# Clearing the send buffer of a mixture-of-experts kernel: one fill of the whole buffer, or 128 zero rows behind each expert's last row

## The reference

```python
gate_scores = einsum('bsd,de->bse', x, gate_w) + gate_b          # 24 experts
topk_val, topk_idx = lax.top_k(gate_scores, 2)
sparse_gates = softmax(topk_val)
combine = sum(one_hot(topk_idx, 24) * sparse_gates[..., None], axis=-2)
h = gelu(einsum('bsd,edf->besf', x, w1) + b1)                    # 128 -> 512, each expert
y = einsum('besf,efd->besd', h, w2) + b2                         # 512 -> 128
out = einsum('bse,besd->bsd', combine, y) + x
```

## Time and profile before

| | |
|---|---|
| median of 3 runs | 788.13 us |
| span of the profiled execution (first to last instruction) | 791.8 us |
| PE / DVE / ACT / POOL busy | 81% / 67% / 51% / 52% |
| DMA traffic over the span | 84.4 MB, of it 45.5 MB written to DRAM |
| Mamba stage | scan from 70 us, its last step at 180 us |
| first mixture | first send at 213 us, first slot loaded from 266 us, results read back from 382 us |
| second mixture, behind the attention | first send at 604 us, first slot loaded from 657 us |

### The profile page before, as it was taken

How to read it: one execution, slowest core, us unless ns; L and a number is a source line. 1 busy time by engine, 2 the same in 40 slices (tenths; PEclk the granted TensorE clock), 3 DMA queues, 4 the chain that set the end, 5 groups by cost and what they waited for, 6 DMA issues and landing times.

```text
span 791.8 us, 17837 instructions
## 1 busy us (share of the span) xinstructions
PE 642.2 (81%) x4583; PEld 434.2 (55%) x4583; DVE 529.6 (67%) x1518; ACT 405.3 (51%) x880; POOL 414.8 (52%) x488
## 2 busy tenths in 40 slices
PE   4974888888865599999287799999888648999890
PEld 2311333324653499999143355555456517999890
DVE  6779999996565266555378889899645633665444
ACT  2645777772321165665075567677644303566550
POOL 5203999985667255454277534444444672545450
PEclk9965999999995799999699599999999867999995
DMA  7979999922011122221618311211002112222215
GB/s 205 321 254 256 251 247 249 249 58 80 8 34 47 53 81 70 72 72 41 185 36 287 128 51 49 59 49 35 4 0 98 34 53 58 78 71 67 67 42 166
DMA packets 88312, 84.43 MB, mean 107 GB/s; under 512 B 12897, under 2 KB 77401, under 8 KB 87977
## 3 DMA queue, kind: packets, MB, share of 16 engines
q1 hardware_dynamic: 82600, 71.89, 33.9%
q0 software_dynamic: 5632, 11.58, 4.5%
HBM read 37.98 MB, written 45.46 MB: 105 GB/s over the span
## 4 chain that ended last, share of the span: by engine, by line
PE 33%; DVE 7%; issue 5%; DMA 2%; SPq 2%; ACT 2%; POOL 1%; ACTq 0%; DVEq 0%; POOLq 0%
PE bank L643 7%; PE bank L652 6%; PE bank L2017 5%; PE bank L1948 3%; PE bank L1951 2%; DVE t_peak L1768 2%; PE bank L2127 2%; PE bank L1993 2%; PE bank L2118 1%; DVE X L249 1%; PE bank L636 1%; SPq L1427 1%; DMA work<-results 1%; PE bank L2044 1%; DVE t_tabs L1848 0%
## 5 line engine op out<-in xcount | busy, mean ns | idle before, releaser
L806 POOL TENSOR_TENSOR UN<-work 128x512 f32<-128x512 f32 x64 | 81.7, 1289 | 55.4 <-DVE work L1034 54.7
L1768 DVE TENSOR_REDUCE t_peak<-bank 128x1 f32<-128x512 f32 (+2 forms) x192 | 104.0, 592 | 9.5 <-PE bank L1951 7.4
L445 ACT ACTIVATE t_v_tiles<-bank,t_e_b1all 128x128 f32<-128x128 f32 x224 | 64.0, 368 | 63.5 <-PE bank L643 58.8
L445 ACT ACTIVATE m_dx_tiles<-bank,m_e_b1all 128x128 f32<-128x128 f32 x224 | 64.0, 369 | 60.0 <-PE bank L643 57.8
L410 POOL DMA_INDIRECT results<-t_A,t_e_to_row x56 | 53.8, 961 | 67.1 <-DVE t_A L559 33.0
L410 POOL DMA_INDIRECT results<-m_XC,m_e_to_row x56 | 53.8, 961 | 63.7 <-issue 33.9
L1181 PE MATMUL bank<-UN,ident 128*128 128x512 f32 x128 | 71.0, 637 | 14.2 <-POOL UN L806 13.6
L1034 DVE TENSOR_TENSOR_SCAN work<-bank,work 128x512 f32<-128x512 f32 x64 | 76.6, 1216 | 8.3 <-POOL UN L806 7.0
L549 DVE COPY UN<-w1all 128x512 f32 x112 | 48.2, 430 | 40.5 <-PE bank L643 28.4
L652 PE MATMUL bank<-w2all,t_v_tiles 128*128 x448 | 60.6, 279 | 2.7 <-ACT t_v_tiles L445 2.0
L643 PE MATMUL bank<-t_A,UN 128*128 128x128 f32 x448 | 61.0, 280 | 0.0
(11 more groups left out here) (323 smaller groups left out, 1441.8 us busy)
## 6 DMA issues: line engine op xcount, KB each, us to landing
xrows<-m_nothing SPq DMA_DIRECT2D x25, 1032.0 KB, 17.9
w1all<-in_e_w SPq DMA_DIRECT2D x6, 1024.0 KB, 12.2
work<-results SPq DMA_DIRECT2D x16, 256.0 KB, 4.5
m_dx_tiles<-xrows SPq DMA_DIRECT2D x56, 64.5 KB
t_v_tiles<-xrows SPq DMA_DIRECT2D x56, 64.5 KB
t_tabs<-stacks SPq DMA_DIRECT2D x32, 96.0 KB, 2.2
work<-stacks SPq DMA_DIRECT2D x32, 96.0 KB, 2.1
m_tabs<-in_e_b SPq DMA_DIRECT2D x1, 1536.0 KB
```

The costliest lines, as they stand in the source:

```text
L445: ins = act.activation(e.hid[:, mp, f * P:f * P + P], core.tiles(2 + mp)[:, f, :], ACT.Gelu, bias=row(e.b1all, x)[:, f:f + 1])
L806: g.tensor_tensor(hc[:, k % 4, :], h[:, k % 2, :], c_sb[:, k % 2, :], ALU.mult).then_inc(hc_ready, 1)
L1768: v.tensor_reduce(peak[p][:, a, ss[0]:ss[-1] + 1, qt], bank[:, f, 0:len(ss) * w].rearrange("p (j n) -> p j n", n=w), AX_X, ALU.max).then_i ...
```

## The change

SP's 25 fills of 1 MB are gone. Each layer now clears only the 128 rows behind each expert's last row, 24 transfers of 66 KB, once the counts are known.

- DVE gets one more instruction in each layer: `end_row` = count + region base, 24 numbers, in front of the chain that works out the slots. It signals `end_row_ready`.
- SP clears for the experts with even numbers and ACT for those with odd numbers (`clear_ends`): wait for `end_row_ready`, then twelve times a `value_load` of the row number and a DMA from `nothing` to `xrows`. On SP this stands in front of the wait for `sent`; on ACT it stands in front of the exponential of the gates (`gexp`).
- SP then waits for `zeroed` to reach the count of all transfers of this layer, before it loads the first slot. POOL's wait for `zeroed` is gone.
- One more static transfer clears the 128 rows that all unused slots now read: `first_row` is capped at that row (DVE, same place, another operation).
- A region is 2176 rows instead of 2048, the buffer 52,352 rows instead of 56,320, and `nothing` is one row of 129 floats per partition, kept over both stages.

The diff, without the declarations of new tiles and semaphores:

```diff
-REGION = NB * T
-XROWS = NE * REGION + SLOT_TILES * P
-ZERO_ROWS = 2
-ZERO_LOADS = NE + 1
+REGION = NB * T + P
+XROWS = NE * REGION + P
...
+    def clear_ends(self, eng, experts):
+        e, core = self, self.core
+        eng.wait_ge(e.end_row_ready, 1)
+        for x in experts:
+            r = eng.value_load(e.end_row[0:1, x:x + 1], min_val=0, max_val=XROWS - P)
+            eng.dma_start(core.xrows[bass.ds(r, P), :], core.nothing[:]).then_inc(core.zeroed, 16)
+
     def sync(self, sp):
         e, core = self, self.core
+        e.clear_ends(sp, range(0, NE, 2))
+        sp.wait_ge(core.zeroed, 16 + 16 * NE * e.layer)
         sp.wait_ge(core.sent, 16 * TOPK * NT * e.layer)
         sp.wait_ge(e.first_row_ready, 1)
...
         if b == 0 and k == 0 and 0 in tiles:
-            g.wait_ge(e.core.zeroed, 16 * ZERO_LOADS)
             g.wait_ge(e.numbered, TOPK)
...
     def scalar(self, act):
         e, core = self, self.core
+        e.clear_ends(act, range(1, NE, 2))
         act.wait_ge(e.gdiff_ready, 1)
...
         count = bank[0:SLOT_TILES, 6, 0:NE]
+        v.tensor_tensor(e.end_row[:], count[0:1, :], e.base_e[0:1, :], ALU.add).then_inc(e.end_row_ready, 1)
...
-        v.tensor_copy(e.first_row[:], begins[0:1, :]).then_inc(e.first_row_ready, 1)
+        v.tensor_scalar(e.first_row[:], begins[0:1, :], float(NE * REGION), None, ALU.min).then_inc(e.first_row_ready, 1)
...
-            for x in range(ZERO_LOADS):
-                rows = core.xrows[x * REGION:min(x * REGION + REGION, XROWS), :]
-                n = rows.shape[0] // P // ZERO_ROWS
-                sp.dma_start(rows.rearrange("(p a r) d -> p a (r d)", p=P, r=ZERO_ROWS),
-                             nothing[:].unsqueeze(1).to_broadcast([P, n, ZERO_ROWS * ROW])).then_inc(core.zeroed, 16)
+            sp.dma_start(core.xrows[NE * REGION:, :], core.nothing[:]).then_inc(core.zeroed, 16)
```

More of the change, by code:

```diff
@@ L71, in __init__ @@
         self.zeroed, self.sent = self.sem("zeroed"), self.sem("sent")
+        self.nothing = self.sb("nothing", [P, ROW])
         self.results = nc.dram_tensor("results", ((TOPK * NT + SLOT_TILES) * P, D), F32).ap()
@@ L280, in __init__ @@
         self.owner, self.first_row = sb("owner", [1, SLOT_TILES], I32), sb("first_row", [1, SLOT_TILES], I32)
+        self.end_row = sb("end_row", [1, NE], I32)
         self.filled, self.emptied = sb("filled", [P, SLOT_TILES]), sb("emptied", [P, SLOT_TILES])
@@ L322, in __init__ @@
         self.gdiff_ready, self.gexp_ready, self.gate_step = map(sem, ("gdiff_ready", "gexp_ready", "gate_step"))
-        self.stored = sem("stored")
+        self.stored, self.end_row_ready = sem("stored"), sem("end_row_ready")
         self.slot_turned, self.xsT_ready, self.w1_ready, self.mm1_done, self.gelu_done = \
@@ L680, in mamba @@
     X1 = core.XN
-    nothing = st.sb("nothing", [P, ZERO_ROWS * ROW])
     spare = core.UN[:].rearrange("p t d -> p (t d)")
@@ L790, in _ @@
                 g.memset(x[:, 0:NCONV - 1], 0.0).then_inc(edge_set, 1)
-            g.memset(nothing[:], 0.0).then_inc(nothing_set, 1)
+            g.memset(core.nothing[:], 0.0).then_inc(nothing_set, 1)
             g.wait_ge(core.consts_set, 1)
```

## The result

The changed kernel takes 790.43 us (median of 20 runs, 787.79 to 793.8), the kernel before 786.29 us beside it (783.64 to 789.38). The ratio is 1.0051 (95% interval 1.0038 to 1.0065): about 4.0 us slower, where no change was forecast.

A forecast was written before the change was run, and what follows sets the result against it. POOL's sends were taken to bound both mixtures' beginnings. Fills 0 (−0.3 at best), DVE 0 and hidden transfers 0 summed to 0 us against the profiled 791.8 us, 788.1 us for the runs' median; range 786.0 to 792.5 us.

The forecast's parts named there:

- What bounds the kernel: Beginning of both mixtures: POOL's sends end last, not the row numbers; SP and PE go on together after the last lands.
- The fills cost nothing: Scan: nobody waits for a fill, so removing them gives 0, at best −0.3 us.
- The sign that I had set against this term: Scan on POOL: rounds shorter than 6.9 us without the fills would mean the fills' term failed.
- DVE: Slots' chain: `end_row` adds 0.20 us a layer, covered by sends that end 13 us later; sum 0.
- The issuing: SP and ACT queues: first clear after 1.75 us, then 1.10 us each, hidden with 1.5 us to spare; cost 0.
- Do the DMA engines carry it?: Clears beside sends: a clear takes 0.27 us of all 16 engines, 65% load, so the issuing sets the pace.
- The far end of the range: Clears at the fills' packet price, 72 ns: landed 3.4 us late in each layer, +6.8 us, 794.9 us.
- The first rival: SP's wait for `zeroed` before the first slot: clears come in late, 3.6 us in all, 791.7 us; chance 0.32.
- The second rival: First slot's group on SP: slots come 1.0 us sooner in each layer, 2.0 us, 786.1 us; chance 0.22.

The follow-up runs named there:

- e18: Changed kernel with the whole buffer still filled in the first layer in rows of 1032 bytes, second run: ratio to the kernel before 1.0055.
- e16: The changed kernel again, unaltered, on one chip beside e18: ratio to the kernel before 1.0068.
- e5: Kernel before, fills kept and no clears, with only the tile `nothing` allocated ahead of `work`: ratio to the kernel before 0.9971.
- e10: Changed kernel with `nothing` allocated after the core's other tiles, so `work` stays at its old address: ratio to the kernel before 1.0074.
- e11: Changed kernel with fills of the whole buffer in both layers, written as rows of 516 bytes: ratio to the kernel before 1.0613.
- e12: Kernel before, fills kept, with 24 loads of 128 rows of 516 bytes at the clears' places: ratio to the kernel before 0.9996.
- e3: Changed kernel with each clear as 16 packets of 4128 bytes from partitions 0 to 15: ratio to the kernel before 1.0065.
- e8: Changed kernel with each clear as 16 packets of 4128 bytes from every eighth partition: ratio to the kernel before 0.9997.
- e13: Changed kernel with each clear as 64 packets of two rows (1032 bytes) from every second partition: ratio to the kernel before 1.0019.
- e4: Kernel before, unaltered, in a second trace: span 786.6 us.
- e2: Kernel before, fills kept, with the 24 clears added but of 16 rows each instead of 128: ratio to the kernel before 0.9988.
- e7: Kernel before, fills kept, with 12 full clears added instead of 24, six on each queue: ratio to the kernel before 0.9993.
- e6: Kernel before, fills kept, with 24 clears of only the first 256 bytes of each row: ratio to the kernel before 1.0011.

## Why the prediction was wrong

**What bounds the kernel: right.** POOL's sends end last at both mixtures' beginning, before and after.

**The fills cost nothing: right, as far as the runs tell.** On one chip e18 (with fills) and e16 (without) can't be told apart. The sign that I had set against this term, shorter rounds in the scan, did not come: 6.88 and 6.87 us for 6.90 and 6.88. The scan as a whole did get shorter, by 1.5 us. The 1.2 us of it near the beginning are there in e5 (fills kept) and e10 (no fills) too, and the rest goes with the moved tile: e5, with all its fills, takes the same 96.5 us as the kernels without them.

**DVE: right.** `end_row` takes 0.16 us for 0.20.

**The issuing: right in sum, in part by luck.** SP's twelfth clear was forecast 261.05 − 247.2 = 13.85 us behind `end_row`; it was issued at 257.03 (244.07 + 13.29 − 0.33), 13.97 us behind it (243.06). Two misses cancel: the first issue came after 1.01 us for 1.75, and SP's groups take 12.96 / 11 = 1.18 us for 1.10. ACT's take 12.14 / 11 = 1.10 us. ACT's table is ready 11 us before its first GELU.

**"Do the DMA engines carry it?": here the prediction failed.** The step priced a clear like a slot's load, 0.27 us of 16 engines, came to a load of 65%, and took from it that the issuing sets the pace and that `sent` comes as before. For the first five to six microseconds of the train that is what the trace shows, even a little less: 27 ns a packet and 58% from 247 to 251 us. What failed is to take the price of single transfers for a train that goes on for 13 us. It asks for about 172 GB/s, and rows of 516 bytes are written at no more than 146 GB/s for long (e11). At that rate a clear takes 144 × 56.5 ns / 16 = 0.51 us, and two of them every 1.10 us are 93% of the engines before a send is counted. From 251 us on the clears' packets take 59 to 61 ns and the sends' 0.294 × 4 us × 16 / 87 = 216 ns for 108 ns (0.162 × 4 us × 16 / 96). The loads of e12 have the slot load's direction and never come to this. So the term put at nothing, the landing of the sends, measured 5.6 − 2.4 = 3.2 and 5.9 − 2.5 = 3.4 us.

The sum by bytes is short: 24 clears and the 13 sends beside them are 2.45 MB, at 146 GB/s 16.7 us from 244.0 on, to 260.7 us. The packets were through at 261.4. It gives the packets' part of the delay to within 0.7 us, and not the 1.3 us that came behind them. The far end of the range had the size, 3.4 us a layer, from the fills' packets: its 72 ns are close to e11's 68 ns by the same count. That its sum came out right to 0.2 us is in part luck, since it let that price hold from the first clear on and knew nothing of the time behind the packets. The row that I should have gone by was in hand: a long write to the same tensor from the same kind of tile.

By the Trainium skill ("DMA: Bandwidth & Descriptors", section "Issuing engines are not separate DMA queues"), issuing from two engines saves only the sequencers' time. The trace agrees: the two queues' trains ran side by side in 13.4 us, where one queue would take 24 × 1.10 = 26 us (an estimate from ACT's pace; no run has it), and their packets went through the same engines as the sends'.

**The first rival had the size but not the mechanism.** It said that SP would wait for `zeroed` behind a slow train of issues. The train was on time. What came late were the sends themselves, which share the engines with the clears; PE waits for `sent` alone, and SP goes on with it. Only e3, and in a small part e8 and e13, showed the rival's own form.

**The second rival was mis-sized.** The 1.0 us that the first slot's group took longer belonged to that one execution. In e4 and e5 the first issue stands 0.9 to 1.0 us behind the release, after the clears 0.7 us: 0.3 us a layer instead of 1.0.

**The moved tile was not seen at all.** The changed kernel declares `self.nothing` ahead of `self.work`; the prediction has no term for what that does to an address.

The account against an ordinary trace of before: +3.2 + 3.4 (landing) − 2 × 0.3 (first group) − 0.3 to 0.8 (moved tile, in the scan) = +5.2 to +5.7 us, beside 786.29 × 0.0051 = 4.0 us measured (3.0 to 5.1). With the 2.3 us of e5's run time in the tile's place it is 3.7 us. The account closes to about 1 us, no better. Its first term, which e2, e7 and e12 take away, is where the forecast's nothing went.

## What to carry to other kernels

Price an added transfer by rows of its own direction, packet size and source layout, and of its own length: a few transfers can go through at a price that a long train of them does not keep. Compare the bytes asked for per microsecond with the rate of a long row of the same kind, and count everything that is under way with it: a background write that is itself in time can still delay the transfer that others wait for. When such a write must be made, give it fewer and longer packets, spread over the partitions (e8), or make less of it (e2, e7). And look at what a new tile does to the addresses of the tiles behind it; a faster instruction is worth only what lies on the path.

## What the runs showed of the hardware

- Long writes of 516-byte rows to DRAM went at 146 GB/s over all 16 engines (56.5 ns a packet, e11), of 1032-byte rows at 250 GB/s (65 ns). Why 516 bytes are so dear was not tried; rows of exactly 512 bytes would be the next run.
- Beside the sends, written packets of 516 bytes took 25 to 35 ns for the first five to six microseconds of a train that asked for 172 GB/s, and 59 to 61 ns after that (251 to 255 us). Packets of 1032 bytes with as many bytes stayed at 39 to 40 ns (e13), pieces of 256 bytes went from 17 ns to 62 to 73 ns after ten microseconds (e6), and reads of 516 bytes stayed at 30 to 40 ns in windows of 4 us (e12). What takes in the first microseconds' writes is not shown.
- PE went on 0.5 to 0.6 us after the last packet of the last send in the kernel before, e2, e8 and e12, and later after it beside the clears: 1.8 and 1.0 us in the changed kernel, 1.1 in e16, 2.0 in e6 (first mixture), 2.1 in e13 (second).
- Packets of 4128 bytes from partitions 0 to 15 held the engines over twice as long (34.6% against 15.9%) as from every eighth partition.
- POOL's 128 × 512 product took 1268 to 1272 ns or 1290 to 1300 ns by where the tile of its inputs begins: by the tiles' sizes, 32 bytes off a multiple of 64 or on one.
